# Attention and mixture of experts on one core: LayerNorm folded into the scores, the first chunk by batches, the opening reordered

## The reference, cut to what matters

```
x   = x + xattn(layernorm(x), ctx)
x   = x + ffn(layernorm(x))

xattn(q, k):  query = q @ Wq.T ; key = k @ Wk.T ; value = k @ Wv.T
              sim  = query @ key.T                       # per batch 256 x 256
              sim  = (sim - mean(sim)) * rsqrt(var(sim) + 1e-5)   # over the whole batch
              out  = softmax(sim) @ value @ Wo.T
ffn(x):       one shared expert + 8 routed experts, swiglu, 128 -> 2*128 -> 128
              probs = softmax(x @ gate_w + gate_b); the best 2 of 8 weigh the experts' outputs
```

## Time and profile before

| | us |
|---|---|
| median of 3 runs | 169.08 |
| lowest and highest | 166.66, 170.59 |
| the profiled execution's own time | 166.58 |
| its span in the trace | 164.5 |
| TensorE busy / VectorE / ScalarE / GpSimd | 138.6 / 112.9 / 69.4 / 23.5 |
| share of the chain that ended last: PE / DVE / ACT / issue | 61% / 14% / 12% / 5% |
| mean granted TensorE clock | 0.969 of full |

### The profile page before, as it was taken

One profiled execution on the slowest core, in us unless ns is written; L12 is line 12 of the kernel. 1 busy time (PEld: TensorE's weight loads), 2 busy tenths in 40 slices (PEclk: granted clock), 3 DMA queues, 4 the chain that ended last, 5 costly groups with the idle time before them and its releaser, 6 DMA issues.

```text
span 164.5 us, 2040 instructions
## 1 busy us (share of the span) xinstructions
PE 138.6 (84%) x625; PEld 99.5 (60%) x625; DVE 112.9 (69%) x339; ACT 69.4 (42%) x129; POOL 23.5 (14%) x39
## 2 busy tenths in 40 slices
PE   0787681269799999987999999969999998999991
PEld 0563571167568777655787787646876764766650
DVE  1679377637778759786879398866498586756651
ACT  3342593068421541189505413596123139412221
POOL 2385134600330200012002000100010000000000
PEclk9999999556999999999999999999999999999999
DMA  3689200000000000000010000000200000020001
GB/s 112 172 232 335 88 0 2 0 4 0 0 0 2 0 0 4 0 2 0 0 64 4 0 0 0 0 2 0 68 0 0 0 0 0 0 68 0 0 2 66
DMA packets 6718, 5.04 MB, mean 31 GB/s; under 512 B 1050, under 2 KB 6707, under 8 KB 6707
## 3 DMA queue, kind: packets, MB, share of 16 engines
q1 hardware_dynamic: 6706, 4.91, 10.2%
HBM read 3.86 MB, written 1.05 MB: 30 GB/s over the span
## 4 chain that ended last, share of the span: by engine, by line
PE 61%; DVE 14%; ACT 12%; issue 5%; POOL 3%; DMA 2%; DVEq 0%; ACTq 0%; POOLq 0%
PE bank L694 55%; DVE xn L498 5%; ACT prob L358 4%; ACT L398 2%; POOL ln_rstd L279 2%; DMA x_sb<-in_x_dram 2%; PE bank L769 2%; ACT L378 2%; DVE ln_stats L484 2%; PE bank L748 2%; POOL w_rest L292 1%; ACT silu L398 1%; PE bank L839 1%; ACT prob_t L368 1%; DVE silu L619 1%
## 5 line engine op out<-in xcount | busy, mean ns | idle before, releaser
L398 ACT ACTIVATE silu<-bank,b_cols 128x512 f32<-128x512 f32 (+1 forms) x37 | 24.9, 677 | 59.7 <-PE bank L694 46.7
L694 PE MATMUL bank<-x_head,w_head 128*128 128x512 f32 x72 | 38.0, 528 | 0.7 <-ACT silu L398 0.7
L619 DVE TENSOR_TENSOR silu<-silu,bank 128x512 f32<-128x512 f32 (+1 forms) x33 | 22.1, 671 | 21.7 <-PE bank L694 21.2
L694 PE MATMUL bank<-act,w_sb 128*128 128x512 f32 (+1 forms) x74 | 36.5, 581 | 0.0
L694 PE MATMUL bank<-x_rest,w_head 128*128 128x512 f32 x72 | 28.8, 399 | 0.0
L694 PE MATMUL bank<-x_head,w_rest 128*128 128x512 f32 x72 | 28.7, 398 | 0.0
L627 DVE SCALAR_TENSOR_TENSOR act<-bank,b_cols,silu 128x512 f32<-128x512 f32 (+1 forms) x37 | 27.2, 736 | 1.7 <-ACT silu L398 0.8
L694 PEld LDWEIGHTS bank<-x_head,w_head 128*128 128x128 f32 x72 | 13.9, 193 | 7.1 <-issue 4.3
L694 PEld LDWEIGHTS bank<-x_rest,w_head 128*128 128x128 f32 x72 | 14.0, 195 | 6.0 <-issue 4.3
L279 POOL TENSOR_TENSOR ln_rstd<-ln_veps,minus_half 128x4 f32<-128x4 f32 x8 | 8.1, 1011 | 61.2 <-DVE ln_veps L491 61.2
L694 PEld LDWEIGHTS bank<-act,w_sb 128*128 128x128 f32 x74 | 13.6, 188 | 3.8 <-issue 0.7
(11 more groups left out here) (106 smaller groups left out, 183.6 us busy)
## 6 DMA issues: line engine op xcount, KB each, us to landing
x_sb<-in_x_dram SPq DMA_DIRECT2D x4, 256.0 KB, 4.8
w_sb<-in_L_ffn_rw_dram SPq DMA_DIRECT2D x1, 1024.0 KB, 5.8
ctx_sb<-in_ctx_dram SPq DMA_DIRECT2D x4, 192.0 KB, 4.4
out_dram<-x SPq DMA_DIRECT2D x3, 256.0 KB, 2.5
w_sb<-in_L_ffn_rw_dram SPq DMA_DIRECT2D x1, 512.0 KB, 7.1
out_dram<-x SPq DMA_DIRECT2D x2, 128.0 KB, 1.8
w_sb<-in_L_ffn_sw_dram SPq DMA_DIRECT2D x1, 128.0 KB, 2.1
wq_sb<-in_L_xattn_Wq_dram SPq DMA_DIRECT2D x1, 64.0 KB, 2.4
```

What stands on the lines that cost most here:

```text
L398: scalar.activation(silu[:, k, cols], HID[(2 * n) % 3][:, cols], ACT.Silu, bias=b1_cols[:, 0, e:e + 1]).then_inc(silu_sb, 1)
L619: dve.tensor_tensor(silu[:, k, cols], silu[:, k, cols], CW_B[:, cols], ALU.mult).then_inc(scaled_sb, 1)
L694: return pe.matmul(dst, lhs, rhs, start=start, stop=stop, skip_group_check=True)
```

## The change

- **LayerNorm folded.** Raw x is transposed (xn of the first norm is gone). The Wk-Wq product is centred over the model dimension (center_qk), which takes the mean of x out; the row's 1/std multiplies moments and exponential scale instead (row_powers holds its powers -0.5 and -1 of var + eps, from one GpSimd instruction). The projection is applied to ctx (u) and not to x (t). Statistics of the scores are per row: four bn_stats of 256 columns a chunk in place of two of 512, then small instructions (scores_moments); the average has 16 columns, summed by scores_variance. Row maxima are taken after the statistics (scores_maxima).
- **Chunk 0 by batches.** u, attention, residual, second statistics, normalise, transposes, heads and rests go by batch j, the second batch in bank[2] (groups, late). Chunks 1 to 3 as before.
- **Opening.** ctx is loaded before x, the four attention weights by ScalarE's queue, expert weights before the biases; b2 is split last; pick is 16 rows made by one VectorE instruction (before: GpSimd fills and a ScalarE cast); fills of cw_t and b2_rows are gone. transpose_prob(1) moves from ahead of slot 0 to behind its hidden matmuls; split_heads of experts 3-5 moves behind router_exp(0).
- **EARLIER = 2.** The pieces of chunk 1 are two slots earlier than the tables say. x_t, ctx_t and u_sb have two buffers.

```diff
         OPENING = {("exponentials", 1), ("transpose_prob", 1), ("prob_copies", 1), ("router_exp", 0)}
+        EARLIER = 2
-                    if where == place and (c - 1) * NX + slot == n and (piece, c) not in OPENING]
+                    if where == place and (c - 1) * NX + slot - (EARLIER if c == 1 else 0) == n and (piece, c) not in OPENING]
...
+        def groups(c):
+            return [[0], [1]] if c == 0 else [[0, 1]]
+        def upto(c, g):
+            return g + 1 if c == 0 else c + CB
+        def late(c, g):
+            return bank[2] if c == 0 and g == 1 else LATE
...  SP
+            load_ctx(0)
             load_x(0)
-            for dst, src in ((wq_sb, wq), (wk_sb, wk), (wo_sb, wo), (wv_sb, wv)):
-                sp.dma_start(dst[:, :], src).then_inc(attn_w_in, 16)
-            load_ctx(0)
             load_x(1)
             load_ctx(1)
...  GpSimd
+            def first_rstd(c):
+                pool.wait_ge(ln_var[0], c + 1)
...
+                pool.tensor_tensor(row_powers[:, c % 2], ln_veps[:, 0, :].unsqueeze(1).broadcast_to([P, 2, TC]),
+                                   powers[:, :, :], ALU.pow).then_inc(ln_r[0], 1)
...
-            pool.memset(cw_t[:, :, :].bitcast(F32), 0.0).then_inc(consts_ready, 1)
-            wait_own(pool.memset(pick_f[:, :, :], 0.0))
...
+            first_rstd(0)
+            first_rstd(1)
             scores_rstd(0)
             split_rests(0, 2)
+            second_rstd(0, 0)
+            second_rstd(0, 1)
             scores_rstd(1)
+            split_rests(2, 3)
...
             for n in range(NX * C):
                 for piece, c in due(POOL_AT, n, 0):
                     pieces[piece](c)
+                if n in (0, 1):
+                    split_rests(3 + n, 4 + n)
+                    if n == 1:
+                        split_rests(5, 6)
                 for piece, c in due(POOL_AT, n, 1):
                     pieces[piece](c)
...  ScalarE
+            for dst, src in ((wk_sb, wk), (wq_sb, wq)):
+                scalar.dma_start(dst[:, :], src).then_inc(qk_in, 16)
+            for dst, src in ((wo_sb, wo), (wv_sb, wv)):
+                scalar.dma_start(dst[:, :], src).then_inc(vo_in, 16)
+            ctx_copy(0)
+            x_copy(0)
+            u_copy(0)
...
+            ctx_copy(1)
+            x_copy(1)
             v_copy(0)
+            u_copy(1)
...
+            split_heads(0, 1)
+            split_heads(1, 2)
+            exponentials(0)
             v_copy(1)
             prob_copy(0)
             prob_copy(1)
...
+            split_heads(2, 3)
             x2_heads(0)
             exponentials(1)
             prob_copy(2)
             prob_copy(3)
             router_exp(0)
+            split_heads(3, 5)
             split_heads(5, 6)
...  VectorE
+            def center_qk():
+                dve.wait_ge(qk_ps, 1)
+                own(dve.tensor_reduce(qk_sum[:, :], bank[1][0:DC, 0:D], X, ALU.add))
+                wait_own()
+                dve.tensor_scalar(qk_t[:, :], bank[1][0:DC, 0:D], float(D), qk_sum[:, :], ALU.mult, ALU.subtract).then_inc(qk_ready, 1)
+            def scores_moments(c):
+                wait_own()
+                own(dve.tensor_tensor(sim_sq[:, :, :], sim_stats[:, :, :, 1], sim_stats[:, :, :, 1], ALU.mult))
+                wait_own()
+                own(dve.scalar_tensor_tensor(sim_ex2[:, :, :], sim_stats[:, :, :, 2], 2.0 / S, sim_sq[:, :, :], ALU.mult, ALU.add))
+                dve.wait_ge(ln_r[0], c + 1)
+                own(dve.tensor_tensor(sim_mom[:, 0], ...row_powers..., ALU.mult))
+                wait_own()
+                dve.tensor_tensor(sim_mom[:, 1], ...row_powers..., ALU.mult).then_inc(simstat_sb, 1)
...
+            dve.tensor_tensor(pick[:, :, :], ident[0:2 * E, 0:E]..., ident[0:2 * E, E:2 * E]..., ALU.add).then_inc(pick_ready, 1)
+            dve.wait_ge(x_in[0], 16)
+            ln_moments(0, 0, x_sb, range(0, IB))
+            center_qk()
+            ln_moments(0, 0, x_sb, range(IB, TC))
+            ln_variance(0, 0, range(TC))
+            first_statistics(1)
             for c in range(2):
+                scores_statistics(CB * c)
+                scores_statistics(CB * c + 1)
+                scores_moments(c)
+                scores_maxima(CB * c)
+                scores_maxima(CB * c + 1)
+                if c == 0:
+                    scores_variance(0)
+                    scores_scale(0)
+            for g in range(CB):
+                residual(0, g)
+                second_statistics(0, g)
             scores_variance(1)
+            for g in range(CB):
+                second_normalise(0, g)
             scores_scale(1)
             x2_rests(0)
...
+            def statistics_1(c):
+                scores_statistics(CB * c + 1)
+                scores_moments(c)
+                scores_maxima(CB * c + 1)
...  TensorE
+            def project_u(c):
+                pe.wait_ge(ctxt_sb, c + 1)
+                for g, js in enumerate(groups(c)):
+                    mm(u_bank(c, g)[:, batch_cols(js)], qk_t[:, :], ctx_t[:, c % 2, batch_cols(js)]).then_inc(u_ps, 1)
...
+            transpose_ctx(0)
+            pe.wait_ge(qk_in, 32)
+            mm(bank[1][0:DC, 0:D], wk_sb[:, :], wq_sb[:, :]).then_inc(qk_ps, 1)
+            transpose_x(0)
+            pe.wait_ge(qk_ready, 1)
+            project_u(0)
+            pe.wait_ge(vo_in, 32)
             pe.transpose(bank[0][:, 0:D], wo_sb[:, :], ident[:, :]).then_inc(setup_ps, 1)
+            scores(0)
...
+            transpose_ctx(1)
+            transpose_x(1)
             project_v(0)
+            project_u(1)
             scores_average(0)
+            scores(1)
             project_v(1)
...
             scores_average(1)
             transpose_x2(0)
             router(0)
-            transpose_prob(1)
...  in the loop over slots
                 hidden(c, e, 1)
+                if n == 0:
+                    transpose_prob(1)
                 run(n, 2)
```

More of the change, by code:

```diff
@@ L174, in early, with values, upto_batch, done @@
             return bank[3:5] if c == 1 else PROB
+        def values(c):
+            return bank[2 - c] if c <= 1 else PROB[0]
+        def groups(c):
+            return [[0], [1]] if c == 0 else [[0, 1]]
+        def upto(c, g):
+            return g + 1 if c == 0 else c + CB
+        def upto_batch(c, j):
+            return j + 1 if c == 0 else c + CB
+        def done(c):
+            return c + CB
+        def batch_tiles(js):
+            return range(IB * js[0], IB * (js[-1] + 1))
+        def batch_cols(js):
+            return slice(S * js[0], S * (js[-1] + 1))
+        def u_bank(c, g):
+            return bank[2] if c == 0 and g == 1 else early(c)[1]
+        def late(c, g):
+            return bank[2] if c == 0 and g == 1 else LATE
+        def weights_bank(c):
+            return CW_B if c == 0 else LATE
         def average(c):
@@ L489, in ln_statistics, with second_normalise @@
                 if c >= 1:
-                    dve.wait_ge(ln_r[which], c)
-                dve.tensor_scalar(ln_veps[:, which, :], ln_mv[:, which, :, 1], EPS, None, ALU.add).then_inc(ln_var[which], 1)
-            def ln_normalise(which, c, src, transposed):
-                dve.wait_ge(ln_r[which], c + 1)
-                if c >= 1:
-                    dve.wait_ge(transposed, c)
-                for i in range(TC):
-                    last = dve.tensor_scalar(xn[:, which, i, :], src[:, TC * c + i, :], ln_mv[:, which, i, 0:1],
-                                             ln_rstd[:, which, i:i + 1], ALU.subtract, ALU.mult)
-                last.then_inc(xn_ready[which], 1)
+                    dve.wait_ge(ln_r[which], c if which == 0 else done(c - 1))
+                t = slice(ts[0], ts[-1] + 1)
+                dve.tensor_scalar(ln_veps[:, which, t], ln_mv[:, which, t, 1], EPS, None, ALU.add).then_inc(ln_var[which], 1)
+            def second_normalise(c, g):
+                dve.wait_ge(ln_r[1], upto(c, g))
+                if c >= 1:
+                    dve.wait_ge(x2t_ps, done(c - 1))
+                for i in batch_tiles(groups(c)[g]):
+                    last = dve.tensor_scalar(xn[:, i, :], x1[:, TC * c + i, :], ln_mv[:, 1, i, 0:1],
+                                             ln_rstd[:, i:i + 1], ALU.subtract, ALU.mult)
+                last.then_inc(xn_ready, 1)
             def scores_statistics(m):
@@ L508, in scores_statistics, with scores_maxima @@
                     dve.wait_ge(negmax_sb, m // CB)
-                own(dve.tensor_reduce(row_max[:, j, :], scores[:, :].rearrange("p (i k) -> p i k", i=IB), X, ALU.max))
-                own(dve.bn_stats(sim_stats[:, j, :], scores[:, :]))
+                for i in range(IB):
+                    own(dve.bn_stats(sim_stats[:, IB * j + i].rearrange("p h k -> p (h k)"), scores[:, i * S:(i + 1) * S]))
+            def scores_maxima(m):
+                j = m % CB
+                own(dve.tensor_reduce(row_max[:, IB * j:IB * (j + 1)],
```

(2 more changed lines are left out.)

378 lines of the change are left out of this document (184 added, 194 removed).

## The result

The changed kernel takes 181.69 us in the median of four runs (179.28 to 182.82), the kernel before 167.94 beside it: a ratio of 1.0755, 95% interval [1.0514, 1.0997]. It is slower. The forecast was 161.9, range 158.8 to 165.8. The profiled execution of the changed kernel took 179.28 us with a span of 177.1, so 18.4 more than the sum of 160.9 made for a profiled execution. Both kernels spend 2.1 to 2.2 us outside the span.

A forecast was written before the change was run, and what follows sets the result against it. Bound: a 41 us opening of dependent steps, then a TensorE-bound body. Opening -8.1, body +2.4 on the profiled 166.58 gives 160.9; plus 1.0 for the median's spread, 161.9 us. Range 158.8 to 165.8.

The forecast's parts named there:

- sum of 160.9: Whole kernel, profiled execution: 166.58 us before, less 8.1 in the opening, plus 2.4 in the body.
- still streams 512 columns, so I take no gain (bounds 0 and 1 us over 32): Body, spread matmuls: contracting 16 rows changes nothing in time; gain 0, at most 1 us, no loss considered.
- rival 1: Opening: clock falls in idle stretches before 23.5 and before the Silu at 32.7; costs 2 to 2.5 us, 164.2; chance 0.18.
- no half-clock stretch: Expected sign in the profile: the clock column shows no stretch at half rate.
- three signs: Forecast wrong if: clock column shows a half, fourth xn tile takes over 1 us, or first Silu comes after 35.
- The opening: Start to first Silu: 4.8 us gained to the exponentials, 3.4 to the xn transposes, 0.1 lost after; 8.1 us earlier.
- rival 2: Second normalise: VectorE loses the port lock it shares with GpSimd; 1.1 us more, 163.0; chance 0.2.
- near miss: Second normalise: GpSimd's subtract starts at about 23.9, VectorE's last tile at about 23.8; lost, it costs about 1.1 us.
- The first Silu: End of the opening: Silu at 32.7, 9.15 us after the xn transposes where it took 9.0 before.
- rival 5: Before first Silu: clock falls and gaps in the slots keep it down; slower than before, 174 us; chance 0.04.
- The stall in slot 8: Body: with EARLIER = 2, TensorE's spread waits 3.0 us for VectorE's scaling, delayed by router_weights.
- What it gives back: Slot 10: the wait for exponentials shrinks by 0.3 us, and 0.25 ahead of it; body net +2.4.

The follow-up runs named there:

- e2_before16: The kernel before with its pick, cw_t and b2 tiles cut from 128 to 16 rows, nothing else changed: 177.94 us, ratio to before 1.0623.
- e1_rows128: The changed kernel with pick, cw_t and b2 tiles back at 128 rows, the added rows zero: 169.41 us, ratio to before 1.0006.
- e9_warm3: e8_warm_early0 with one more unread matmul before the router product and four instead of three in slot 1: 159.99 us, ratio to before 0.9581.
- e8_warm_early0: e5_warm with EARLIER = 0, chunk 1's router steps back in their old slots: 161.2 us, ratio to before 0.968.
- e5_warm: e1_rows128 plus three unread matmuls in each of TensorE's two long idle stretches of the opening: 165.14 us, ratio to before 0.9917.

## Why the prediction was wrong

**The step that failed** is the sentence on the body that a contraction of 16 rows "still streams 512 columns, so I take no gain (bounds 0 and 1 us over 32)". The columns were right: a second spread of 16 rows costs 0.23, like any other matmul of 512 columns, and the load takes 0.18 for 0.19. But the step priced the matmul by itself. In the row of loads of before one could have seen that the load of the spread starts with the matmul in front and that of the pair behind it under the spread. No row of that trace shows spreads of fewer rows, so the loss could not be read from it, but neither could the bound of 0 on that side. By hindsight, two loads of 0.19 no longer hidden are 0.38 a spread, 12 us for 32 (an estimate). Measured, the rows cost the body 12.5 us in e2_before16: up to 0.39 for a spread, and 0.3 for a pair of b2 matmuls (0.98 from the matmul before to the one behind at 48.62 to 49.60, where e1_rows128 has 0.68 at 148.82 to 149.50). That is 12.5 of the 18.4 us. None of the five rivals had it: the one on the slower side was the clock.

The second step that failed is the clock: rival 1, and the forecast's "no half-clock stretch". Two of the three signs that the prediction named for being wrong came: the clock column shows a half, and the first Silu comes after 35.

**The opening** held up to the transposes. First exponential 14.88 (forecast 14.6), pow of eight numbers 1.65 us (1.6), transposes of xn 23.91 (23.55), with the four xn tiles in 1.11 us, so the lock of rival 2 was not lost there. GpSimd and VectorE did meet, one instruction later. VectorE of the changed kernel:

```profile
23.26 1.11 DVE L558 TENSOR_SCALAR xn<-x,ln_mv,ln_rstd 128x128 f32<-128x128 f32 x4
24.45 1.23 DVE L607 TENSOR_TENSOR row_scale<-row_powers,sim_r 128x4 f32<-128x4 f32 x1
...
25.78 0.75 DVE L636 TENSOR_TENSOR x_rest<-bank,x_head 128x256 fp32r<-128x256 f32 x2
```

and GpSimd:

```profile
24.39 1.27 POOL L338 TENSOR_TENSOR w_rest<-w_sb,w_head 128x512 fp32r<-128x512 f32 x1
```

The step of 4 numbers a row, 0.16 us at 14.00, lasts until the subtract beside it is through. (So does one of 32 numbers at 34.65, 1.70 us beside a subtract of 1.81, off the path.) The near miss was called for the right stage and the wrong instruction, and it was lost: x_rest stands behind that step and ends at 26.53, and the router's product, which waits for it, starts at 26.63, 2.72 us behind the transposes and not the 2.05 of the forecast. By x_head, ready at 25.53, it could have started about 0.6 earlier (an estimate).

**The first Silu** is where the opening lost its gain: forecast 32.7, measured 36.66. From the transposes it took 12.75 us and not 9.15. With full clock all the way, in e9_warm3, it took 9.88 (24.46 to 34.34). So 2.9 of the 3.6 is what rival 1 priced at 2 to 2.5. The remaining 0.7 is the late start of the router's product, which is 2.72 behind the transposes in e9_warm3 too. The rival's chance was 0.18, argued from idle stretches being shorter than the 4 us that passed in the earlier trace rows; it came true in both stretches that it named, of 3.48 and of 3.2 us. The clock stayed at half from 37.5 to 44.2, over the second half of slot 1 and the attention of chunk 1 behind it, which rival 5 described in kind, though for 7 us only. One row of a clock that fell after 4 us idle had been read as if it excluded a fall after 3.5.

**The stall in slot 8** was right in its place and cause, 2.16 and 2.78 us where 3.0 was forecast; VectorE's router_weights end at 71.24, the scaling follows at 71.32, the spread at 72.05. Slots of 2.87 in place of 2.49 shorten it: with 128 rows it is 2.78. What it gives back was near: the waits in slots 9 and 10 shrink by 0.70 between e8_warm_early0 and e1_rows128, forecast 0.55. What the stall does to the clock behind it (e5_warm, e1_rows128) was not thought of.

**The sum.** 18.4 us are missed in the profiled execution. 12.5 are the rows. At the first Silu the kernel is 4.0 late (2.9 of clock, 0.7 at the router's product, 0.4 before it). From there to the first spread it takes 3.77 us at half clock, where before took 2.86: 0.9. The attention of chunk 1 takes 3.34 at half clock (41.15 to 44.49, above), where before has 1.70:

```profile
49.40 1.95 PE L694 MATMUL bank<-v_sb,prob_t 128*128 128x128 f32 x16
51.10 0.48 PE L694 MATMUL bank<-x_head,w_head 128*128 128x512 f32 x1
```

That is 1.6 more. The stall was 0.8 less than forecast. Together 18.2, of which the clock has 5.4. The range of 158.8 to 165.8 missed by 16 us, mainly because a term of 32 repetitions had been given no side for a loss. A slip beside it: by the prediction's own parts the chance of faster adds up to 0.86, not 0.83.

Without the rows the forecast would still have missed: e1_rows128 takes 169.41 and is no faster than the kernel before, at a forecast of 161.9. That e9_warm3's 159.99 lies near the sum without the stall, 158.5, is in part luck: it has unread matmuls that nobody forecast.

## What to carry to other kernels

Before a tile of a matmul is made smaller, look at the weight loads around it: where each load starts under the matmul before it, a tile of 16 to 64 rows among ones of 128 lost two hidden loads here, and the zero-filled tile of full height was the cheaper one. Multiply a price that you can't see by how often it is paid before you call it zero; 0.39 us in a loop of 32 was worth more than the whole reordering of the opening. Work that was brought forward on one engine left TensorE idle elsewhere, and that idle stretch had a second price in the clock behind it: read both, and try unread matmuls in the gap where nothing useful fits.

## What the runs showed of the hardware

- A matmul contraction of 16, 32 or 64 rows between ones of 128 costs up to 0.39 us more per excursion (0.09 in front, 0.19 behind, 0.11 at the pair after that; 512 columns, full clock), the same at each of these heights; a second one of few rows behind the first costs the usual 0.23. That its cost did not end with the next matmul was not expected, and why the pair after it still pays 0.11 stays open.
- In the changed kernel the granted clock fell to half at 23.91, when TensorE started again after 3.48 us idle, and at about 37.5, just after it started again from 3.17 us idle. In e5_warm it fell at 65.5, 2.4 us into the wait in slot 8 (the last matmul ends at 63.09), but it did not fall in or behind the 2.16 us of the same wait in the changed kernel. In e5_warm it fell at 27.8 as well, with TensorE busy, behind idle stretches of 0.81 and 1.77 us.
- In e9_warm3 eight unread matmuls in the opening, in idle stretches that they didn't fill (0.81, 0.90 and 0.38 us stayed), went with a full clock for the whole of four executions out of six.
- A VectorE step of 4 numbers a row, 0.16 us elsewhere, took 1.23 us beside a GpSimd subtract of 1.27 us, and one of 32 numbers, 0.19 elsewhere, 1.70 beside 1.81.
